# Values by way of main memory: one transfer out and four back, in place of sixteen on the chip

## The reference, cut to what matters

```python
def _L0_attn_ref(hidden, Wq, Wk, Wv, Wo):
    q, k, v = proj(hidden, Wq), proj(hidden, Wk), proj(hidden, Wv)   # b, head, token, 16
    scores = jnp.einsum('bhqd,bhkd->bhqk', q, k) * scale + bias      # bias: -inf outside the window of 64
    attn = jax.nn.softmax(scores, axis=-1)
    out = jnp.einsum('bhqk,bhkd->bhqd', attn, v)
    out = out.transpose(0, 2, 1, 3).reshape(B, S, D)
    return jnp.einsum('bsd,ed->bse', out, Wo)

def _L0_ffn_ref(x, W1, b1, W2, b2):
    Wq1, Wq2 = _quantize(W1), _quantize(W2)          # -1, 0, 1
    h = jax.nn.relu(jnp.einsum('bsd,fd->bsf', x, Wq1) + b1)
    return jnp.einsum('bsf,df->bsd', h, Wq2) + b2

x = x + _L0_attn_ref(_layernorm(x), Wq, Wk, Wv, Wo)
x = x + _L0_ffn_ref(_layernorm(x), W1, b1, W2, b2)
```

## Time and profile before

| | |
|---|---|
| median of three runs | 708.03 us |
| the profiled execution | 706.77 us |
| its span, first to last instruction | 705.0 us |
| TensorE busy, share of the span | 94% |
| ScalarE | 90% |
| VectorE | 89% |
| GpSimd | 85% |
| the 16 DMA engines, queue of SyncE | 45.3% |
| mean granted clock of TensorE | 0.983 |

### The profile page before, as it was taken

How to read it: one execution, slowest core, us unless ns; L and a number is a source line. 1 busy time by engine, 2 the same in 40 slices (tenths; PEclk the granted TensorE clock), 3 DMA queues, 4 the chain that set the end, 5 groups by cost and what they waited for, 6 DMA issues and landing times.

```text
span 705.0 us, 24654 instructions
## 1 busy us (share of the span) xinstructions
PE 666.0 (94%) x8168; PEld 566.0 (80%) x8168; DVE 627.2 (89%) x1596; ACT 637.2 (90%) x2680; POOL 598.3 (85%) x836
## 2 busy tenths in 40 slices
PE   8677879999999999999999999999999999997896
PEld 5465668888888888988888888888888888887785
DVE  5699898999999998999999899999999898888764
ACT  4889989999999999999999999999999998998832
POOL 8288998898989999898989989898988989889820
PEclk9879999999999999999999999999999999999999
DMA  8765544464564555474565546465554546361000
GB/s 297 109 97 65 108 39 76 71 96 78 73 112 69 91 90 69 84 98 76 72 110 72 79 91 82 85 88 88 71 108 47 78 73 74 80 69 29 17 31 31
DMA packets 430773, 57.65 MB, mean 82 GB/s; under 512 B 403380, under 2 KB 422198, under 8 KB 430648
## 3 DMA queue, kind: packets, MB, share of 16 engines
q1 hardware_dynamic: 419784, 46.97, 45.3%
q10 hardware_dynamic: 10864, 9.11, 4.5%
HBM read 12.00 MB, written 8.39 MB: 29 GB/s over the span
## 4 chain that ended last, share of the span: by engine, by line
ACT 33%; PE 28%; POOL 15%; issue 13%; DVE 8%; DMA 1%; SPq 1%; ACTq 0%; POOLq 0%; DVEq 0%
ACT p L462 16%; POOL p L363 7%; PE ps L1041 6%; PE ps L988 5%; POOL tl L387 5%; ACT xnC L489 4%; PE ps L951 3%; PE ps L931 3%; PE ps L1014 3%; ACT xnA L479 3%; ACT hTh L539 3%; PE ps L999 3%; DVE negm L678 2%; POOL th L381 2%; PE ps L1053 2%
## 5 line engine op out<-in xcount | busy, mean ns | idle before, releaser
L462 ACT ACTIVATE p<-ps,negm 128x96 f32<-128x96 f32 x1024 | 343.0, 383 | 12.9 <-DVE negm L678 12.9
L387 POOL TENSOR_TENSOR tl<-pt,th 128x384 f16<-128x384 f32 x256 | 235.7, 921 | 50.4 <-ACT th L471 38.8
L462 ACT ACTIVATION_READ_ACCUMULATOR p<-ps,negm 128x1 f32 x1024 | 255.2, 251 | 0.0
L363 POOL TENSOR_TENSOR p<-p,rden 128x384 f32<-128x384 f32 x256 | 212.3, 829 | 11.2 <-DVE rden L685 9.4
L691 DVE STREAM_TRANSPOSE pt<-p 128x384 f32<-128x384 f32 x256 | 141.7, 554 | 12.2 <-POOL p L363 10.4
L678 DVE TENSOR_REDUCE negm<-ps 128x4 f32<-128x384 f32 x256 | 135.6, 530 | 8.6 <-PE ps L931 6.3
L931 PE MATMUL ps<-k,qbd 128*128 128x96 f16 x2048 | 130.0, 207 | 0.0
L931 PEld LDWEIGHTS ps<-k,qbd 128*128 128x128 f16 x2048 | 116.5, 98 | 13.4 <-issue 0.6
L951 PE MATMUL ps<-th,vb 128*128 128x96 f16 (+1 forms) x1120 | 98.7, 204 | 5.7 <-POOL tl L387 4.8
L951 PEld LDWEIGHTS ps<-th,vb 128*128 128x128 f16 x1120 | 93.3, 99 | 8.5 <-POOL tl L387 8.5
L951 PE MATMUL ps<-tl,vb 128*128 128x96 f16 (+1 forms) x1120 | 98.2, 203 | 0.0
(11 more groups left out here) (136 smaller groups left out, 1412.2 us busy)
## 6 DMA issues: line engine op xcount, KB each, us to landing
k<-kst SPq DMA_DIRECT2D x62, 288.0 KB, 4.1
vb<-vd SPq DMA_DIRECT2D x256, 32.0 KB, 2.5
out<-x SPq DMA_DIRECT2D x32, 256.0 KB, 2.4
qbd<-qs SPq DMA_DIRECT2D x252, 32.0 KB, 2.4
x<-in_L_attn_hidden ACTq DMA_DIRECT2D x15, 512.0 KB, 5.1
vb<-in_L_ffn_W SPq DMA_DIRECT2D x2, 1024.0 KB, 7.9
k<-kst ACTq DMA_DIRECT2D x2, 288.0 KB, 4.3
x<-in_L_attn_hidden SPq DMA_DIRECT2D x1, 256.0 KB, 3.2
```

Of the source, the lines that this page charges most:

```text
L363: e.tensor_tensor(p3, p3, rden[n % 4][:, :].unsqueeze(2).to_broadcast([128, 4, 96]), ALU.mult).then_inc(s_nm, 1)
L387: e.tensor_tensor(tl[g % 2][:, o], pt[n % 3][:, :], th[g % 2][:, o], ALU.subtract).then_inc(s_lo, 1)
L462: ins = e.activation(p[:, 96 * u:96 * u + 96], bank[:, 96 * u:96 * u + 96], ACT.Exp, bias=m[:, u:u + 1], accum_out=r[:, u:u + 1])
```

## The change

A scratch tensor `scr` in main memory is added, of two slots (chunks of even and odd number) with 32 x 4 rows of 2048 numbers (4096 bytes). At position 13 `keep_v` writes the whole of `vd` there in one transfer of 512 KB, 128 rows of 4096 bytes; before it SyncE waits for the place of chunk c-2 to be done, which read that scratch slot. At position 14 `place_v` waits until the scratch is written, and issues four transfers, one per head h, from the scratch into `vb`: 32 partitions by 128 pieces of 32 bytes, 4096 pieces or 128 KB each. The number and size of the pieces that land in `vb` stay as they are. ScalarE's wait before it writes `vd` is now on the transfer into the scratch, and the values product waits for 64 a use and not 256.

```diff
+        scr = nc.dram_tensor("scr", (2, 32, 4, 2048), f16, kind="Internal").ap()
...
+        d_scr = sem("d_scr")
...
-            def place_v(c, m):
+            def keep_v(c):
+                e.wait_ge(s_alo, 8 * c + 6)
+                if c >= 2:
+                    e.wait_ge(d_v[(c - 2) % 3], 64 * ((c - 2) // 3 + 1))
+                e.dma_start(scr[c % 2].rearrange("p m x -> m p x"),
+                            vd[:, :, :, :, :, :].rearrange("p t g v h d -> p (t g v h d)")).then_inc(d_scr, 16)
+
+            def place_v(c):
                 b = c % 3
-                e.wait_ge(s_alo, 8 * c + 6)
+                e.wait_ge(d_scr, 16 * (c + 1))
                 e.wait_ge(s_zv, min(c, 2) + 1)
                 if c >= 3:
                     e.wait_ge(s_pv, 4 * (c - 1))
                 for h in range(4):
-                    src = vd[32 * m:32 * m + 32, :, :, :, h, :].rearrange("p t g v d -> p (t g v) d")
-                    dst = vb[b][32 * h:32 * h + 32, m, :, :, :, h, :].rearrange("p t g v d -> p (t g v) d")
-                    e.dma_start(dst, src).then_inc(d_v[b], 16)
+                    e.dma_start(vb[b][32 * h:32 * h + 32, :, :, :, :, h, :].rearrange("p m t g v d -> p (m t g v) d"),
+                                scr[c % 2].rearrange("p m (x h d) -> p (m x) h d", h=4, d=16)[:, :, h, :]
+                                ).then_inc(d_v[b], 16)
...
                 c = spread(n, V_DMA, 17)
                 if c is not None:
-                    for m in range(4):
-                        place_v(c, m)
+                    keep_v(c)
+                c = spread(n, V_DMA + 1, 18)
+                if c is not None:
+                    place_v(c)
...
-                    e.wait_ge(d_v[(c - 1) % 3], 256 * ((c - 1) // 3 + 1))
+                    e.wait_ge(d_scr, 16 * c)
...
-                e.wait_ge(d_v[c % 3], 256 * (c // 3 + 1))
+                e.wait_ge(d_v[c % 3], 64 * (c // 3 + 1))
```

## The result

The changed kernel takes 781.73 us (781.04 to 784.05), 1.1045 times the kernel before, 95% interval 1.1015 to 1.1075: 73 us slower. The forecast was no change, 707.0 us; that the time lies inside the stated range of 703 to 785 us is owed to the rivals and not to the forecast. The profiled execution took 781.98 us, its span is 780.2 us.

A forecast was written before the change was run, and what follows sets the result against it. TensorE (94% busy) and the other compute engines were the limit, with transfers hidden and queries barely in time. Steady chunks summed to 0, first chunk and end to about nothing: 707.0 us, no change, range 703 to 785.

The forecast's parts named there:

- SyncE's shorter work: Sixteen issues removed from SyncE's queue, 15.1 us a chunk: worth nothing by itself, only lets keys and queries be issued sooner.
- The half microsecond of slack of the queries: Queries, behind the values in SyncE's queue, land at 363.5 to 364.2; TensorE asks at 364.5 for group 2's scores.
- the way out: One 512 KB transfer to the scratch, issued at 338.1, taken to land after 5.1 us, low end 2.4.
- rival 2: Outgoing transfer on only four DMA engines lands after 8 us, narrowing the queries' slack; chance 0.44 together with rival 1.
- what stands behind the way out: After the scratch is written: values land 11.1 us later, queries another 5.6 us later, run without gaps, at 359.9.
- slack of 4.6 us: Queries predicted on the chip at 359.9 against 364.5 needed; holds until a piece costs 13 ns.
- The price of a piece: A 32-byte piece read from main memory on the way back: 8.5 ns, so four transfers need 8.7 us.
- the line through two rows of main memory: From 1 KB in 46 ns and 4 KB in 164 ns: 7 ns a piece without bytes, 8.5 ns for 32 bytes.
- rival 1: Queries late before group 2's scores, from dear pieces: 744 us at 15.4 ns; chance 0.44 together with rival 2.
- The first chunk: Chunk 0's values land at 44.4, first values product at 45.98: nothing, or a few tenths either way.
- The clock: Granted clock might dip behind TensorE's waits; otherwise waits were translated one-to-one into time.
- Rival 2's sum for 15.4 ns: Four-engine way out and pieces at 15.4 ns together: 5.4 us a chunk, x 15 = 81 us, 788 us.

The follow-up runs named there:

- out4: The changed kernel with the way out cut into four transfers of 32 partitions, scratch, bytes and rows the same: 710.52 us, ratio 1.004.

## Why the prediction was wrong

**What bounded the kernel before: right.** The transfers were hidden, and SyncE's shorter work was worth nothing: no variant gained. The half microsecond of slack of the queries, read from SyncE's queue and TensorE's timeline, was the thing on which all turned. The wait named as the place, before the scores of group 2, is where the time went.

**The step that failed is the way out.** "I take 5.1" was the time of a load of 512 KB; measured: 11.7 us in that chunk, 10.1 to 11.7 in all, because four of the sixteen engines carried it. With sixteen, in out4, it is 3.5 to 6.6 us, mostly 3.6, so that the row chosen would have been fair for such a transfer; it was the wrong row for this one. The text held the mechanism as rival 2 and called it likely, yet left it out of the forecast, which was the fault. Its price was too low as well: 8 us, of it 5.0 for the rows at 26 GB/s an engine, where by the packet records the rows took 10.0 us from first to last in that chunk and 8.5 in the last one, with no load of x beside.

**A second step was missized:** what stands behind the way out. From the scratch written to the queries on the chip it was 342.13 to 362.07, 19.9 us, where the sum had 11.1 + 5.6 = 16.7. The values were down after about 12.2 us, not 11.1, and the queries about 7.7 us later, not 5.6. "Now run without gaps" is what failed there: SyncE could pass to the keys only at 350.34, 8.2 us after the scratch was written and not 3.3; the first of the two key issues then held it for 3.0 us, the eight of the queries took 6.2 us, and the last of these landed 2.2 us after its issue. An issue of the way back took 2.3 us in the median (560 to 3712 ns), against 0.75 in the sum. It is not the size of a transfer alone: of the four in this chunk, all of 4096 pieces, the first took 0.58 us and the others 2.2 to 2.7. I take it that SyncE is held by the transfers that it has already issued. The two errors, 6.6 and 3.2 us, turn a slack of 4.6 us into 5.2 us too late; TensorE asked 0.7 us later than before (27.2 us after the values' first issue, 26.4 before) and waited 4.5.

**The price of a piece: right.** 8.5 ns by the line through two rows of main memory, 9.05 recorded; its bytes do not matter down to 16. Part of this is luck: the line was worked with rounded numbers, and without rounding it gives 45.8 - 39.5 + 1.2 = 7.5 ns. The Trainium skill's section "Why small descriptors are slow (HBM only)" (page "DMA: Bandwidth & Descriptors"), which spoke against the change (its place is rival 1, not the second as the prediction has it), does not decide it: 9.05 ns against 7.2 on the chip is a quarter more in recorded time, and the way back alone costs nothing in a steady chunk.

**The first chunk: wrong** for the same reason, 44.4 predicted for the values, while the first values product waited 6.9 us.

**The clock** was only named as a possibility. The translation of waits into time was not one to one: 4.9 us lost for 3.8 us of waiting, and the clock is the likely reason.

**Rival 2's sum for 15.4 ns** (5.4 us a chunk, 788 us) came near the result by errors that offset each other: its pieces were too dear, its way out too short, its issues too quick. The 15.4 ns had been left over for the query pieces after the other rows were subtracted; in the trace's packet records of the kernel before a query piece takes 9.9 ns on the mean, and the long rows more than the 1240 us allowed.

## What to carry to other kernels

Before a transfer is made larger, look at the outermost size of both its sides: the kernel wrote 512 KB to a target walked as 4 blocks of 32 rows, and four of sixteen DMA engines did it, in 10 to 12 us; four transfers of 32 rows each did the same in 3.6 us in most chunks. Count how late the last thing in the same queue may come, here half a microsecond, before fewer instructions there are called a gain; and where a slow transfer stands in a shared queue, removing the wait for it does not remove its cost. A chance called likely in the working belongs into the forecast.

## What the runs showed of the hardware that I had not expected

- A small piece is recorded with about 9 ns from main memory, with 32 bytes (9.05 ns) as with 16 (8.97 ns); on the chip it was 7.2 ns. These times overlap on an engine: in full slices a piece is done every 5.9 ns, and with the pauses every 9.2 to 10.6.
- How long SyncE is held by an issue depends on what it has issued before: 0.58 us for the first of four transfers of 4096 pieces and 2.2 to 2.7 us for the next three; 5.6 us for a transfer of 1024 pieces with a slow one ahead, where the median is 0.67.
- Two transfers with an outermost size of 2, issued together, keep only two engines busy in all (share 0.13), not four.
- The packets of 4 bytes behind a transfer tell on how many engines it ran: 4, 16, and 2 for each of two.
- A row of 4 KB took 161 to 253 ns on sixteen engines, 226 on four and 185 on two: the number of engines does not set it.
